# A two-layer graph block on one Trainium2 core: the degree phase from the largest strip to the smallest, with degrees and scaled tiles in four batches and half of the first normalisation on GpSimd

## The reference

```python
h = jnp.maximum(_layernorm(x), 0.0)
# layer 0
HW = h @ W0
A_norm = relu((A + A.T) * 0.5)
D = A_norm.sum(axis=1)
d = D ** -0.5  (0 where D is 0)
L_norm = eye(N) - d[:, None] * A_norm * d[None, :]
x = x + relu(L_norm @ HW)
# layer 1
h = jnp.maximum(_layernorm(x), 0.0)
y = diag(A) @ (h @ W1[0]) + triu(A, 1) @ (h @ W1[1]) + tril(A, -1) @ (h @ W1[2])
x = x + y + bias
```

## Time and profile before

| what | us |
|---|---|
| three runs | 1035.67, 1029.00, 1033.26 |
| median of them | 1033.26 |
| the profiled execution | 1033.5 |
| its span in the profile | 1031.7 |

### The profile page before, as it was taken

One profiled execution on the slowest core, in us unless ns is written; L12 is line 12 of the kernel. 1 busy time (PEld: TensorE's weight loads), 2 busy tenths in 40 slices (PEclk: granted clock), 3 DMA queues, 4 the chain that ended last, 5 costly groups with the idle time before them and its releaser, 6 DMA issues.

```text
span 1031.7 us, 17707 instructions
## 1 busy us (share of the span) xinstructions
PE 950.0 (92%) x4614; PEld 795.6 (77%) x4614; DVE 576.9 (56%) x1491; ACT 497.5 (48%) x1058; POOL 293.3 (28%) x289
## 2 busy tenths in 40 slices
PE   4787879989989998999999999899999999999998
PEld 4776668777877877878787888678888888888886
DVE  5895656677666676566555666444334333433332
ACT  5986455566565565444444444424333333333331
POOL 4685233333433433344444444201001100000000
PEclk9986899999999999999999999999999999999999
DMA  8995588898888986555555555556666655555552
GB/s 236 324 334 136 194 255 267 274 314 271 291 305 266 302 291 206 165 178 167 133 168 173 171 150 161 169 186 208 186 189 190 181 179 170 159 168 168 162 166 74
DMA packets 181210, 213.73 MB, mean 207 GB/s; under 512 B 13616, under 2 KB 116016, under 8 KB 178992
## 3 DMA queue, kind: packets, MB, share of 16 engines
q1 hardware_dynamic: 171952, 196.46, 62.8%
q10 hardware_dynamic: 9216, 16.78, 4.4%
HBM read 145.04 MB, written 68.16 MB: 207 GB/s over the span
## 4 chain that ended last, share of the span: by engine, by line
PE 61%; DMA 13%; issue 8%; ACT 6%; POOL 5%; DVE 5%; SPq 2%; ACTq 0%; DVEq 0%; POOLq 0%
PE psAcc L500 16%; PE psAcc L502 16%; PE psAcc L501 16%; DMA s_dram<-C 5%; DMA xp<-g_dram 3%; POOL colacc L920 3%; DMA xp<-in_x 2%; PE psG L471 2%; DMA t_dram<-x 2%; ACT xp L630 2%; PE psG L473 2%; PE psG L472 2%; POOL n_rs L912 1%; PE psZ L433 1%; DVE hTl L851 1%
## 5 line engine op out<-in xcount | busy, mean ns | idle before, releaser
L560 ACT ACTIVATE Lh<-C 128x512 fp32r<-128x512 f32 x256 | 161.3, 631 | 294.8 <-PE psAcc L502 235.2
L500 PE MATMUL psAcc<-Xh,Lh 128*128 128x512 f32 x512 | 209.3, 409 | 6.6 <-DVE Xl L779 4.7
L502 PE MATMUL psAcc<-Xh,Ll 128*128 128x512 f32 x512 | 202.8, 396 | 0.0
L501 PE MATMUL psAcc<-Xl,Lh 128*128 128x512 f32 x512 | 202.7, 396 | 0.0
L500 PE MATMUL psAcc<-Yh,Lh 128*128 128x512 f32 x512 | 200.9, 392 | 0.0
L502 PE MATMUL psAcc<-Yh,Ll 128*128 128x512 f32 x512 | 200.2, 391 | 0.0
L501 PE MATMUL psAcc<-Yl,Lh 128*128 128x512 f32 x512 | 200.0, 391 | 0.0
L723 DVE TENSOR_TENSOR Ll<-C,Lh 128x512 fp32r<-128x512 f32 x128 | 91.0, 713 | 141.4 <-ACT Lh L560 141.3
L500 PEld LDWEIGHTS psAcc<-Xh,Lh 128*128 128x128 f32 x512 | 98.4, 192 | 25.8 <-issue 7.7
L502 PEld LDWEIGHTS psAcc<-Xh,Ll 128*128 128x128 f32 x512 | 97.9, 191 | 21.7
L501 PEld LDWEIGHTS psAcc<-Xl,Lh 128*128 128x128 f32 x512 | 98.3, 192 | 17.9
(11 more groups left out here) (124 smaller groups left out, 1489.1 us busy)
## 6 DMA issues: line engine op xcount, KB each, us to landing
C<-at_dram SPq DMA_DIRECT2D x128, 256.0 KB, 2.7
at_dram<-AT SPq DMA_DIRECT2D x16, 1088.0 KB, 6.1
R<-in_adj SPq DMA_DIRECT2D x64, 256.0 KB, 5.8
C<-in_adj SPq DMA_DIRECT2D x64, 256.0 KB, 4.2
s_dram<-C ACTq DMA_DIRECT2D x64, 256.0 KB, 4.1
g_dram<-g SPq DMA_DIRECT2D x32, 512.0 KB, 4.7
C<-s_dram SPq DMA_DIRECT2D x64, 256.0 KB, 4.3
xe<-in_x SPq DMA_DIRECT2D x32, 256.0 KB, 3.7
```

The lines of the kernel that those rows point to most:

```text
L500: mm(acc, lh, rh[:, k, :], start=k == 0, stop=False)
L501: mm(acc, lh, rl[:, k, :], start=False, stop=False)
L502: mm(acc, ll, rh[:, k, :], start=False, stop=c < L1 and k == NB - 1).then_inc(used, 1)
L560: A(Lh[:, q, :], C[:, q, :], ACT.Relu if s.c < L1 else ACT.Copy).then_inc(lhi, 1)
```

## The change

- The strips are taken from k = 15 to 0 (CH0 reversed), in i = 15 - k; buffers and semaphores go by i. Tiles of x are taken from 15 to 0 as well, j = 15 - m.
- A table STAGES says which tiles are handled behind which strip: i = 0: 0; 1: 1, 2; 2: 3; 3: 4, 5; 4: 6; 5: 7, 8; 6: 9, 10; 7: 11, 12; 8: 13, 14; 9: 15, 16; 10: 17; 11: 18; 12: 19; then none. (Tiles are j up to 15; the numbers above are only for the later parts of the stages.)
- Column sums, degrees, powers and scaled tiles come in four batches of four strips, 15 to 12 first. Column sums and degrees of batches 0 to 2 stand behind strips i = 4, 8, 12, the power (root) behind 5, 9, 13, the scaled tiles behind 6, 10, 14. Batch 3 is done after the last strip.
- Step 0 takes its quarters from the last to the first (part), with R, C, AT and the scaled tiles indexed to match.
- The normalisation of a tile: ScalarE does two of the four groups, GpSimd the other two by tensor_scalar (subtract mean, multiply by rstd), and the Relu of the transposed tile moves to the reads of psAcc.
- The first quarter of R and C for step 0 is issued behind strip i = 12.

The core of the diff:

```diff
-        CH0 = [(k, g) for k in range(NB) for g in range(k // 4 + 1)]
+        CH0 = [(k, g) for k in reversed(range(NB)) for g in range(k // 4 + 1)]
         BELOW0 = [max(0, min(4, k - 4 * g)) for k, g in CH0]
         ADDS0 = [0]
         for w in BELOW0:
             ADDS0.append(ADDS0[-1] + (1 if w else 0))
-        FIRST0 = [CH0.index((k, 0)) for k in range(NB)] + [len(CH0)]
-
-        def stages(k):
-
-            return (0, 1) if k == 0 else (k + 1,) if k < NB // 2 else (k + 1, k + 2) if k == NB // 2 else (k + 2,)
+        FIRST0 = [CH0.index((NB - 1 - i, 0)) for i in range(NB)] + [len(CH0)]
+        STAGES = [(0,), (1, 2), (3,), (4, 5), (6,), (7, 8), (9, 10), (11, 12), (13, 14), (15, 16), (17,), (18,), (19,),
+                  (), (), ()]
+
+        def part(s, q):
+
+            return NQ - 1 - q if s.c == 0 else q
+
+        def degrees_done(e):
+
+            return FIRST0[4 * e + 4]
+
+        def batch(e):
+
+            return 4 * (NQ - 1 - e)
...
-            for k in range(NB):
-                load0(k)
-            for q in range(NQ):
+            for i in range(NB):
+                load0(i)
+                if i == NB - 4:
+                    load_next(Step(None, 0), 0)
+            for q in range(1, NQ):
...
-            def column_sums():
-
-                pe.wait_ge(p0C, ADDS0[-1] + 1)
-                for j in range(NB - 1):
+            def column_sums(e):
+
+                pe.wait_ge(p0C, ADDS0[degrees_done(e)] + 1)
+                wait(pe, d_sum, e)
+                for j in range(batch(e), min(batch(e) + 4, NB - 1)):
...
+                    if i in (4, 8, 12):
+                        column_sums(i // 4 - 1)
+                    for j in STAGES[i]:
+                        if j >= 4:
+                            times_W0(j - 4)
+                        if 2 <= j < NB + 2:
+                            turn0(j - 2)
...
-            times_W0(NB - 2)
-            rows_T(Step(None, 0), 2)
-            column_sums()
-            rows_T(Step(None, 0), 3)
-            times_W0(NB - 1)
+            column_sums(NQ - 1)
+            for q in range(2, NQ):
+                rows_T(Step(None, 0), q)
...
+            def h0(j):
+                act.wait_ge(s0_nm, j + 1)
+                n0 = n0s[j % 2]
+                m = NB - 1 - j
+                for b in range(HB // 2):
...
+                A(T0[j % 2][0][:, :], psAcc[:, j % 2, :], ACT.Relu).then_inc(t0hi, 1)
...
+            def scaled_hi(e):
+
+                act.wait_ge(d_inv, e + 1)
+                act.wait_ge(hw0, 4 * e + 4)
+                for n in range(batch(e), batch(e) + 4):
+                    A(Xh[:, n, :], hst[:, n, :], ACT.Copy, scale=scal[:, 0, n:n + 1]).then_inc(prep_hi, 1)
...
+                    i = NB - 1 - k
+                    for j in STAGES[i]:
+                        if 1 <= j <= NB:
+                            h0(j - 1)
+                        if 2 <= j < NB + 2:
+                            turned0(j - 2)
+                        if j >= 4:
+                            got_W0(j - 4)
+                    if i in (6, 10, 14):
+                        scaled_hi(i // 4 - 1)
...
+            def degrees(e):
+
+                o = slice(batch(e), batch(e) + 4)
+                dve.wait_ge(p0R, degrees_done(e))
+                V.reduce_sum(d2[:, o], drow[:, o, :], axis=AX.X).then_inc(d_sums, 1)
+                dve.wait_ge(d_sums, e + 1)
+                dve.wait_ge(p0D, e + 1)
+                V.tensor_tensor(d1[:, o], psD[:, o], d2[:, o], ALU.add).then_inc(d_sum, 1)
+                dve.wait_ge(d_sum, e + 1)
+                V.tensor_scalar(d2[:, o], d1[:, o], 0.0, None, ALU.is_le).then_inc(d_none, 1)
+                dve.wait_ge(d_none, e + 1)
+                V.scalar_tensor_tensor(out=dsafe[:, o], in0=d1[:, o], scalar=0.5, in1=d2[:, o],
+                                       op0=ALU.mult, op1=ALU.add).then_inc(d_safe, 1)
+
+            def scaled_lo(e):
+
+                for i in range(4):
+                    n = batch(e) + i
+                    dve.wait_ge(prep_hi, 4 * e + i + 1)
+                    V.scalar_tensor_tensor(out=Xl[:, n, :], in0=hst[:, n, :], scalar=scal[:, 0, n:n + 1],
+                                           in1=Xh[:, n, :].bitcast(F32), op0=ALU.mult, op1=ALU.subtract).then_inc(prep_lo, 1)
...
+                    if i in (4, 8, 12):
+                        degrees(i // 4 - 1)
+                    for j in STAGES[i]:
+                        if 1 <= j <= NB:
+                            mean0(j - 1)
+                        if j < NB:
+                            wait(dve, s0_h, j - 1)
+                            wait(dve, s0_hp, j - 1)
+                            dve.wait_ge(ld_x0[NB - 1 - j], 16)
+                            stats(n0s[j % 2], hst[:, NB - 1 - j, :], s0_st, s0_mv, s0_ve, j + 1)
+                        if 3 <= j < NB + 3:
+                            low0(j - 3)
+                    if i in (6, 10, 14):
+                        scaled_lo(i // 4 - 1)
...
+            degrees(NQ - 1)
+            for q in range(NQ):
+                split_lo(Step(None, 0), q)
+                if q < NQ - 1:
+                    sum_T(Step(None, 0), q + 1)
+            scaled_lo(NQ - 1)
...
+            def root(e):
+
+                o = slice(batch(e), batch(e) + 4)
+                pool.wait_ge(d_safe, e + 1)
+                power(scal[:, 0, o], dsafe[:, o], mhalf[:, 0:4]).then_inc(d_inv, 1)
...
+                    i = NB - 1 - k
+                    if i in (5, 9, 13):
+                        root(i // 4 - 1)
+                    for j in STAGES[i]:
+                        if j < NB:
+                            n0, m = n0s[j % 2], NB - 1 - j
+                            pool.wait_ge(s0_ve, j + 1)
+                            power(n0.rs[:, :], n0.ve[:, :], mhalf[:, 0:HB]).then_inc(s0_rs, 1)
+                            pool.wait_ge(s0_rs, j + 1)
+                            for b in range(HB // 2, HB):
+                                f = slice(b * F, (b + 1) * F)
+                                last = G.tensor_scalar(hst[:, m, f], hst[:, m, f], n0.mv[:, b, 0:1], n0.rs[:, b:b + 1],
+                                                       ALU.subtract, ALU.mult)
+                            last.then_inc(s0_hp, 1)
+            root(NQ - 1)
```

More of the change, by code:

```diff
@@ L375, in by_W0, with turn0 @@
                 return last
-            def turn0(m):
-                pe.wait_ge(s0_h, m + 1)
-                wait(pe, t0hi, m - 1)
-                wait(pe, t0lo, m - 1)
+            def turn0(j):
+                pe.wait_ge(s0_h, j + 1)
+                pe.wait_ge(s0_hp, j + 1)
+                wait(pe, t0hi, j - 1)
+                wait(pe, t0lo, j - 1)
                 for b in range(HB):
                     f = slice(b * F, (b + 1) * F)
-                    last = nc.tensor.transpose(psAcc[:, m % 2, f], hst[:, m, f], ident[:, :])
+                    last = nc.tensor.transpose(psAcc[:, j % 2, f], hst[:, NB - 1 - j, f], ident[:, :])
                 last.then_inc(t0, 1)
@@ L549, in copy_T @@
                     wait(act, st_at[s.c % 2], s.pair(0, 16))
-                A(AT[:, s.c % 2, q * Q:(q + 1) * Q], psA[:, q % 2, :], ACT.Copy).then_inc(at_ok, 1)
+                A(AT[:, s.c % 2, part(s, q) * Q:(part(s, q) + 1) * Q], psA[:, q % 2, :], ACT.Copy).then_inc(at_ok, 1)
             def split_hi(s, q):
@@ L561, in split_hi @@
                 if s.c < NB:
-                    act.dma_start(strip(s_dram, s, 0, q), C[:, q, :]).then_inc(st_s[q], 16)
+                    act.dma_start(strip(s_dram, s, 0, part(s, q)), C[:, q, :]).then_inc(st_s[q], 16)
             for n, (k, g) in enumerate(CH0):
@@ L713, in sum_T @@
                 wait(dve, ld_c[q], s.of(16, 16))
-                V.tensor_tensor(C[:, q, :], AT[:, s.c % 2, q * Q:(q + 1) * Q], C[:, q, :], ALU.add).then_inc(S_ok, 1)
+                V.tensor_tensor(C[:, q, :], AT[:, s.c % 2, part(s, q) * Q:(part(s, q) + 1) * Q], C[:, q, :], ALU.add).then_inc(S_ok, 1)
             def split_lo(s, q):
@@ L771, in _ @@
-            V.scalar_tensor_tensor(out=dsafe[:, :], in0=d1[:, :], scalar=0.5, in1=d2[:, :],
-                                   op0=ALU.mult, op1=ALU.add).then_inc(d_safe, 1)
-            for q in range(1, NQ):
-                sum_T(Step(None, 0), q)
-                split_lo(Step(None, 0), q - 1)
-            split_lo(Step(None, 0), NQ - 1)
-            for n in range(NB):
-                dve.wait_ge(prep_hi, n + 1)
-                V.scalar_tensor_tensor(out=Xl[:, n, :], in0=hst[:, n, :], scalar=scal[:, 0, n:n + 1],
-                                       in1=Xh[:, n, :].bitcast(F32), op0=ALU.mult, op1=ALU.subtract).then_inc(prep_lo, 1)
+                    if i in (4, 8, 12):
+                        degrees(i // 4 - 1)
@@ L781, in _ @@
+                    if i in (6, 10, 14):
+                        scaled_lo(i // 4 - 1)
+            sum_T(Step(None, 0), 0)
+            degrees(NQ - 1)
+            for q in range(NQ):
```

(18 more changed lines are left out.)

112 lines of the change are left out of this document (37 added, 75 removed).

## The result

The changed kernel took 1062.23 us (median of four executions, 1058.3 to 1064.53), the kernel before 1031.13 beside it: a ratio of 1.0296, interval 1.0238 to 1.0353. That is 31 us slower; 10 were forecast, and the time lies above the range. The profiled execution took 1058.3 us, 24.8 more than the one before. Some executions fall into a slower state of the chip; the ratios leave them out, the medians don't.

What follows compares the result with a forecast made beforehand. TensorE was taken to bound all but the first 121.6 us, where ScalarE leads the degree phase. Step 0 at 115.7 us plus 15.6 put step 1 at 131.3, 10 us later: 1033.3 + 10 = 1043 us, range 1024 to 1054.

Steps and rivals of the forecast that it cites:

- the 90.0 us of the sum: Degree phase added up on GpSimd's queue to the end of strip 6: 13.1 + 33.4 + 30.0 + 6.4 + 2.3 + 4.8.
- start: Degree phase before the first column add: 2.55 MB loaded by 10.7 us, then 2.4 us through transpose, add and Relu: 13.1 us.
- tail: Strips 5 to 0, where the chain goes from engine to engine: 25.7 us, first matmul of step 0 at 115.7 us.
- (e): Two added 128x128 GpSimd operations for each of sixteen tiles: 0.3 us each, 0.6 us a tile, 9.6 us in all.
- The rival with 0.8 us: GpSimd's two new operations cost 0.8 us each: 10 us more, 1053 us; chance 0.15, all slower.
- (f): Added inside the strips: four batches of scalings, three GpSimd roots of 1.15 us, VectorE's column-sum waits in strips 11, 7, 3.
- (g): Tile order, seven strips with two tiles: six two-power strips at 5.0 us on GpSimd's queue, 30.0 us, the dear part.
- (a): Step 0: twelve of sixteen scalings move ahead of it, so the 4.66 us stall for the x tile goes.
- (b): Step 0 after its stall: slow matmuls (0.63 us, warm 0.40) go, saving 2.4 us, and 0.4 for the transposes between.
- (c): Column sums, degrees and powers: three quarters hidden under other work; 1.3 us of sums and one 1.15 us power remain.
- The rule against the change: VectorE and GpSimd operations on SBUF exclude each other: twelve Xl tiles wait up to 1.25 us each, 15 us from above.
- The round trips hide: Rival: GpSimd never waits for VectorE, a double strip costs 3.2 us instead of 5.0; 1023 us, half of it 1033; chance 0.18.

## Why the prediction went right and wrong

The side was right and the place too: all of the loss is made before step 1. The size was not. Step 1 starts 16.2 us later than the 131.3 forecast, and two of the signs that the prediction named for being wrong came: step 0 after 125 us, and an operation of GpSimd over 0.5 us. In the profiled execution the terms of the sum carry that as follows; the 90.0 us of the sum hold the second root and the last tile's operations, which end at 102.5 us, behind the last column add of strip 6 (98.9). A wait within a stage is counted with the stage.

| term | forecast | measured |
|---|---|---|
| start | 13.1 | 15.8 |
| column adds to strip 6 | 33.4 | 33.2 |
| six double stages | 30.0 | 38.0 |
| four single stages | 6.4 | 11.2 |
| two roots | 2.3 | 2.0 |
| other waits | 4.8 | 2.3 |
| tail | 25.7 | 24.6 |
| step 0 | 15.6 | 20.4 |

- *The start* was 2.7 short. TensorE's first transpose waited for the first strip's data until 13.02 us, not 10.7, and every kernel with the new order had its first column add at 15.0 to 17.3 us. The rate was right (325 GB/s from 5 to 10 us), but some 3.2 MB had moved by then and not 2.55 (an estimate from the GB/s of the stretches): further tiles of x were issued right behind the first strip. The order alone, said to cost its load, proved worth 10 us, a third of the change.
- **(e) is the step that failed by its price**: an operation with two pointer scalars takes 0.84 us, not 0.3. A pair is 1.57 us, so an undisturbed double stage took 5.46 us instead of 5.0 and a single one 2.67 instead of 1.6: 7.1 us of the 16.2. The rival with 0.8 us named the right price, and its 10 us were near what the half costs (7); but its 1053 rested on the same base as the forecast.
- **The step that failed by its theory is the sum itself: it ran (f) and (g) on GpSimd's and VectorE's queues and gave TensorE 2.1 us, in the tail only.** Without (e) it would have the last column add of strip 6 end near 85 us, or 88 with the start as measured; the kernel with all of the normalisation back on ScalarE has it at 100.6, behind waits of up to 5.99 us. With the double stages and no half, the waits behind them fell from 12.9 to 5.3 us when only TensorE's work was cut. The forecast had read TensorE's 5.32 of 10 from 90 to 100 us, where it mostly waits for others. Inside the strips the same rows have 7.70 of 10 at a granted clock of 1.00, and at 0.50 the products with W0 follow each other at 0.21 us instead of 0.11: at that clock and with two tiles in a strip nothing of the slack is left.
- *(g), 30 us of double stages as the dear part*: the six took 38.0 us, so dear they are; but taking the table back gave 5 to 8 us. GpSimd's and TensorE's queues are about equally long here: with GpSimd's pairs gone it waits for TensorE, and with TensorE lightened the pairs and the rest of its own work remain.
- *The tail* came out right in total, with a backlog of TensorE in it that wasn't forecast: partly luck.
- *(a) and (b), 7.5 us off step 0*: it took 20.4 us instead of 15.6. The stall stayed, 3.75 us. Moving twelve of sixteen Xl away was not enough, since the fourth batch and the Ll and C of the split (2.0 us a quarter) still stand ahead of the x tile's statistics. With these moved the step took 15.3 us, so its own length was sized right; but the stall of 6.01 us then came in step 1, so nothing of it would have reached the end.
- *(c)*: the last column sums and root took about what was said (1.71 and 1.40 us), but behind a wait: 6.72 us from GpSimd's last column add to the last degrees.
- *The rule against the change* held where it was looked for, but cheaply: the pair beside a row of Xl tiles took 3.05 us instead of 1.57 (at 73.05 us), the one such pair in this trace.
- *Steps after step 1 unchanged*: right in this execution, 24.2 of 25.9 us reached the end. "The round trips hide" fell.
- Two slips of the prediction's arithmetic change nothing: 96 + 15.6 is 111.6 and not 111.3, and the chances of its parts add up to 0.49 within 1% and 0.40 slower, not 0.47 and 0.42.

## What to carry to other kernels

Before work is moved, ask of every engine, not only of the one whose queue is added up, how full it is in the stretches that change, and, for TensorE, what that share would be at 1.2 GHz: here it was the next bound. Price an operation by a row of its own form (operands and scalars), not by a row of its size. And before a stall is removed, look at what the next one waits for: four times the x tile's stall was removed from step 0, and each time it came back in step 1, where a transfer sets the time.

## What the runs showed of the hardware

- GpSimd's tensor_scalar on 128x128 takes 0.84 us with two pointer scalars and about 0.63 us with constants; a one-input operation of the same size takes 0.29 us.
- A 128x1 operation of GpSimd with two inputs took 8.60 us, 100.33 to 108.93, beside thirteen Xl operations of VectorE in a row, 100.18 to 108.87 (the kernel with the x tile moved ahead), and 0.19 to 0.20 us in the fifteen other steps of that run: it ended when VectorE's row did, not with VectorE's first instruction. The Trainium skill (SBUF — State Buffer, Who interferes with whom) has the two engines exclude each other for an instruction; the trace agrees and shows that the loser can wait for a whole row of them. It need not: GpSimd's one-input operations beside such a row took 0.56 to 0.82 us in the kernel before (97.71 to 99.92 us), and 0.29 elsewhere.
- From 110 to 120 us of the kernel with single stages TensorE was busy 10.00 of 10 and the granted clock stayed at 0.50. In the changed kernel it rose within such a row: products with W0 that followed each other at 0.21 us until 97.2 us did so at 0.11 us after it. In step 0 of the changed kernel the 512-column matmuls took 0.63 us each for some 4 us and then 0.39.
